# Sixteen products of every chunk summed on TensorE instead of on GpSimd and VectorE, in a graph network with a selective scan

## The reference, cut to what matters

```
h = relu(adj @ x @ gcn_w + gcn_b); h = layernorm(h) * ln_g + ln_b
xz = h @ w_in;  xc, z = xz[:, :256], xz[:, 256:]
u = silu(causal_conv4(xc) + conv_b)
dbc = u @ w_xp                      # 8 ranks, 16 of B, 16 of C
dt = softplus(dbc[:, :8] @ w_dt + b_dt)
dA = exp(dt[:, :, None] * A);  dBu = dt[:, :, None] * B[:, None, :] * u[:, :, None]
def step(hst, inp):                 # hst: 256 channels x 16 states
    dAt, dBut, Ct = inp
    hst = dAt * hst + dBut
    return (hst, hst @ Ct)          # sum over 16 states of state * C
_, ys = lax.scan(step, zeros, (dA, dBu, C))
out = x + ((ys + u * D_skip) * silu(z)) @ w_out
```

## Time and profile before

| what | value |
| --- | --- |
| median of 3 runs | 2748.58 us (2747.08 to 2750.45) |
| the profiled execution, its own time | 2750.08 us |
| its span in the profile | 2748.1 us |
| PE busy | 2307.8 us (84%) |
| DVE busy | 2213.9 us (81%) |
| ACT busy | 1033.1 us (38%) |
| POOL busy | 977.4 us (36%) |
| first L672 of slot 0 to the last scan of slot 255 | 1508.7 to 2732.0 us |

### The profile page before, as it was taken

The page is one execution under the profiler, slowest core; times in us unless marked ns, Lnnn a source line. Parts: engine busy times, 40 slices in busy tenths (PEclk is TensorE's granted clock), DMA queues, the critical chain, the costliest instruction groups (busy, mean ns, idle before and its releaser), DMA issues.

```text
span 2748.1 us, 22503 instructions
## 1 busy us (share of the span) xinstructions
PE 2307.8 (84%) x6968; PEld 1294.8 (47%) x6968; DVE 2213.9 (81%) x2409; ACT 1033.1 (38%) x1745; POOL 977.4 (36%) x409
## 2 busy tenths in 40 slices
PE   0347788999999999999999888888888988886776
PEld 0222344444458888888874344433333444333333
DVE  5889888877627666656542999999999999999997
ACT  0000000000015555555433555555555555555552
POOL 0000000000000000000000778778777787777554
PEclk9968799999999999999999999999999999997888
DMA  8999999889756555555556555555555564541111
GB/s 337 383 402 410 394 394 381 365 351 369 275 222 238 214 192 217 218 187 202 195 212 256 203 192 194 190 191 195 194 188 213 184 214 177 191 171 69 61 63 58
DMA packets 108326, 643.03 MB, mean 234 GB/s; under 512 B 14224, under 2 KB 15024, under 8 KB 42672
## 3 DMA queue, kind: packets, MB, share of 16 engines
q1 hardware_dynamic: 92160, 604.02, 57.7%
q10 hardware_dynamic: 16048, 37.57, 3.9%
HBM read 625.28 MB, written 16.25 MB: 233 GB/s over the span
## 4 chain that ended last, share of the span: by engine, by line
PE 49%; DVE 34%; issue 13%; ACT 2%; ACTq 1%; DMA 1%; POOL 0%; DVEq 0%; POOLq 0%
PE ps L853 20%; PE ps L771 12%; DVE arena L568 12%; DVE arena L686 7%; PE ps L893 6%; DVE ps L672 5%; PE ps L972 4%; PE ps L934 3%; DVE ring L686 2%; PE ps L793 2%; DVE arena L693 1%; ACTq L1002 1%; DVE arena L731 1%; DVE parts L718 1%; PE ps L914 1%
## 5 line engine op out<-in xcount | busy, mean ns | idle before, releaser
L460 POOL TENSOR_TENSOR rstd<-base,minus_half 128x8 f32<-128x8 f32 (+1 forms) x40 | 85.8, 2144 | 1492.2 <-DVE base L508 924.9
L853 PE MATMUL ps<-adj_parts,h_parts 128*128 128x512 f32 x2592 | 593.6, 390 | 2.5 <-ACT adj_parts L1068 2.1
L893 PE MATMUL ps<-ring,diag_h 128*128 128x512 f32 x1152 | 542.6, 604 | 2.1 <-DVE arena L658 2.0
L476 POOL TENSOR_TENSOR arena<-arena 128x1024 f32<-128x1024 f32 x192 | 461.4, 2409 | 230.7 <-ACT state L1135 229.7
L853 PEld LDWEIGHTS ps<-adj_parts,h_parts 128*128 128x128 f32 x2592 | 484.7, 188 | 108.8 <-ACT adj_parts L1068 4.6
L568 DVE TENSOR_TENSOR arena<-arena,ring 128x2048 f32<-128x2048 f32 x208 | 476.8, 2292 | 64.0 <-DMA ring<-adj 45.8
L771 PE MATMUL ps<-ring,arena 128*128 128x512 f32 x928 | 432.0, 626 | 64.0 <-DMA ring<-adj 64.0
L686 DVE TENSOR_TENSOR_SCAN arena<-arena,state,ps 128x512 f32<-128x512 f32 x384 | 469.4, 1264 | 1.0 <-ACT arena L1143 0.5
L1143 ACT ACTIVATE arena<-arena,a_sb 128x512 f32<-128x512 f32 x512 | 338.6, 709 | 61.7 <-DVE arena L733 61.2
L672 DVE TENSOR_TENSOR ps<-arena,ps 128x512 f32<-128x512 f32 x512 | 327.6, 685 | 19.0 <-PE ps L914 18.0
L893 PEld LDWEIGHTS ps<-ring,diag_h 128*128 128x128 f32 x1152 | 222.6, 196 | 253.2 <-issue 250.1
(11 more groups left out here) (94 smaller groups left out, 1950.6 us busy)
## 6 DMA issues: line engine op xcount, KB each, us to landing
ring<-adj SPq DMA_DIRECT2D x480, 1024.0 KB, 6.5
arena<-c_scratch SPq DMA_DIRECT2D x128, 512.0 KB, 3.8
diag_h<-adj SPq DMA_DIRECT2D x32, 1024.0 KB, 12.2
arena<-x ACTq DMA_DIRECT2D x16, 512.0 KB, 5.1
x_scratch<-arena ACTq DMA_DIRECT2D x8, 512.0 KB, 3.0
arena<-x_scratch ACTq DMA_DIRECT2D x16, 256.0 KB, 4.5
out<-arena ACTq DMA_DIRECT2D x16, 256.0 KB, 3.9
lower_scratch<-arena ACTq DMA_DIRECT2D x7, 512.0 KB, 2.6
```

Of the source, the lines that this page charges most:

```text
L476: nc.gpsimd.tensor_tensor(buf, buf, c_row, ALU.mult).then_inc(mult_done, 1)
L853: last = nc.tensor.matmul(acc[:, c, :], h_parts[:, blk % 2, layer, h_part, a * F:(a + 1) * F], adj_parts[:, buf, adj_part, c * MM:(c + 1) ...
L893: last = nc.tensor.matmul((acc_c if i else y_ps)[:, c, :], tile_of(h1, JT * s + a), blk[:, a * STRIP + c * MM:a * STRIP + (c + 1) * MM], s ...
```

## The change

POOL's pair sums (L480) and DVE's sums of pairs (L693) go, with their semaphores and the constants `QUADS`, `QUAD` and `SPARED`. POOL only multiplies by C. PE sums all sixteen buffers of every chunk, four matmuls in each even slot, as it did before in the last three chunks. The waits for a free `hs` buffer and for the finished sum count pairs now, and stand in the same slots.

```diff
-                    if g % 2 and g // 2 < PAIRS_ADDED:
-                        pool.wait_ge(mult_done, g + 1)
-                        even = hs[(g - 1) % HSB]
-                        nc.gpsimd.tensor_tensor(even, even, buf, ALU.add).then_inc(pair_done, 1)
...
-                        G = (g - HSB) // 2
-                        if added_to_next(G):
-                            dve.wait_ge(quad_done, quads_before(G + 1))
-                        else:
-                            dve.wait_ge(nsum_done, nsums_before(G + 1))
+                        dve.wait_ge(nsum_done, (g - HSB) // 2 + 1)
...
-                G, odd = divmod(g - QUAD, 2)
-                if not odd and 0 <= G < NCH * DS // 2 and added_to_next(G):
-                    dve.wait_ge(pair_done, G + 2)
-                    both = hs[(2 * G + 2) % HSB]
-                    nc.vector.tensor_tensor(both, both, hs[2 * G % HSB], ALU.add).then_inc(quad_done, 1)
...
-                    dve.wait_ge(nsum_done, nsums_before(DS // 2 * (k + 1)))
+                    dve.wait_ge(nsum_done, DS // 2 * (k + 1))
...
+                    pe.wait_ge(mult_done, 2 * G + 2)
+                    if pair == 0 and G:
+                        pe.wait_ge(y_free, G // (DS // 2))
+                    for j in range(2):
+                        for h in range(HALVES):
+                            last = nc.tensor.matmul(y_ps[:, h, :], ident[:, :], hs[(2 * G + j) % HSB][:, h, :],
+                                                    start=pair == 0 and j == 0,
+                                                    stop=pair == DS // 2 - 1 and j == 1)
+                    last.then_inc(nsum_done, 1)
```

More of the change, by code:

```diff
@@ L71 @@
 LOAD_X1, SKIP, GATE, OUT, RESIDUAL = 12, 20, 21, 25, 25
-QUADS = (1, 3)
-QUAD = 6
-SPARED = 3
 F32 = mybir.dt.float32
@@ L340, in build @@
         mult_done = sem("mult_done")
-        pair_done = sem("pair_done")
-        quad_done = sem("quad_done")
         nsum_done = sem("nsum_done")
@@ L370, in dbu_of @@
             return b_ps[g % 2] if h else first_dbu_ps
[L372 to L382, removed]
         weight_loads = [
```

## The result

| | before | after |
| --- | --- | --- |
| median of 4 runs | 2749.5 us (2747.1 to 2755.8) | 2883.8 us (2881.6 to 2889.5) |
| ratio after/before | | 1.0488, 95% interval 1.0465 to 1.0511 |
| span of the profiled execution | 2748.1 us | 2882.6 us |

The change costs 134 us. 2860 with a range of 2820 to 2890 was forecast, so the direction and the range hold and the size is 24 us short. The busy times by stretch say where the time lies: chunk 0, chunks 1 to 11, chunk 12, chunk 13, chunk 14.

The account below looks back on a forecast made before the run. DVE bounds the kernel before; PE would bound the changed one through a loop of 84.0 us plus 2.5 of half clock, 86.5 per chunk. Chunks 1 to 11 +95, with hand-overs, chunks 12 and 0 +111: 2860 us, range 2820 to 2890.

Parts of the forecast that it names:

- The coupling by one slot: PE and DVE, every slot: PE can be late by about one slot at no cost, and early by none.
- rival 1: Looser coupling, PE's work of 79.5 us per chunk bounds only on average: about 2780 us; chance 10%.
- PE's term of the loop: PE, slots 0 to 12: 61.5 instructions, 3.0 rows of B, 3.8 output and small stages, 2.5 half clock.
- the sum: Loop through PE's slots 0 to 13 and DVE's to 15: 84.0 us per chunk, 86.5 with half clock.
- DVE's term: From PE's slot 13 to the next slot 0: 1.35 + 1.7 + 8.8 + 3.8 us.
- 84 to 88 us per chunk as the sign of being right: Chunks 1 to 11 would each take this long if the forecast held.
- a shorter L731, L733 or L752 by a microsecond: DVE instructions: shortening by this much would show that POOL did matter; no gain was taken.
- The relief of VectorE: DVE's removed L693, 3.6 us per chunk: a gain only if DVE stayed the bound.
- The clock: PE behind its idle stretch before slot 0: half clock stays and adds 2.5 us per chunk.
- Chunk 12: 86.5 us plus 3.5 for the last hand-over in slot 13: 90.0 against 78.3, +12.
- Chunk 0: Slots 0 to 3 at DVE's pace, no sum in slot 4: 81 us against 76.9, +4.
- Rival 2: DVE stays the bound, sums slip into PE's waiting, pitch 0.35 us instead of 0.43: 2703 us; chance 4%.

Follow-up runs that it names:

- The kernels with the same work in two places: Kernel before plus 8 zero matmuls per chunk: in slots 14 and 15, 2753.0 us; in slots 7 and 8, 2825.0 us.
- the zero matmuls in the change's own slots: Kernel before plus the change's 20 extra matmuls per chunk, multiplying by zeros, POOL's and DVE's sums kept: 2884.0 us, ratio 1.0477.
- moving the products: Changed kernel with the products with adj spread by weights over a chunk's slots instead of evenly: 2821.0 us, 83.1 us per chunk.
- with POOL's instruction short: Changed kernel with GpSimd multiplying only the first 8 of 512 columns by C: 2814.4 us, 83.4 us per chunk.
- a small transfer of work: Kernel before without VectorE's sums of pairs, four more matmuls per chunk on TensorE: 2752.1 us; with products moved too, 2714.5 us.
- the moving alone: Kernel before with only the products with adj spread by weights over a chunk's slots: 2744.7 us, 76.4 us per chunk.

## Why the prediction was right, and where it was short

- **PE becomes the bound, by its place in the list and not by its average: right.** The coupling by one slot was the argument that set 2860 apart from rival 1's 2780. The kernels with the same work in two places show it directly (+0.1 and +6.2 us per chunk), the zero matmuls in the change's own slots reproduce the whole slowdown, and moving the products takes 5.2 us of 10.4 per chunk back.
- **PE's term of the loop: right.** In chunk 3 PE's slots 0 to 12 take 71.0 us, from the row of B before slot 0 to that of slot 13 at 1836.42; the sum had 61.5 + 3.0 + 3.8 + 2.5 of half clock = 70.8.
- **DVE's term: too small by 1.9 us, and this is the step that was mis-sized.** From PE's row of B in slot 13 to that of the next slot 0 it is 17.5 us in the mean of chunks 1 to 11, where the sum had 15.65. In chunk 3 it is 17.4, from 1836.42 to 1853.79. L701 and L726 were taken as in the rows before, 1.7 us; L669 and L694 take 1842.03 - 1838.14 = 3.9 in this chunk. Slot 14 is 0.8 shorter (7.98 against 8.8) because L699 there escapes with 1.22. That is so in six of the eleven chunks; in the five others, as in chunk 5, L694 takes 1.2, behind its 0.55 of waiting for ACT, and L699 3.1, and the term is 17.7. I asked whether GpSimd would release VectorE and answered no from L733, rightly; I didn't ask which instruction a *shifted* multiplication would now meet. The rest, 0.3 to 0.4 us, lies in slot 13 between the row of B and L669 (1.72 against 1.35): the row of B takes 0.63 there, start to start, against the 0.30 of the earlier trace rows. PE's term was 0.1 too large, so a chunk is 1.8 us over the sum, and 1.8 x 11 is 19 of the 24 us. I had named 84 to 88 us per chunk as the sign of being right; 88.3 lies just outside it. I had also named a shorter L731, L733 or L752 by a microsecond as the sign that POOL matters: none got shorter by that much in the mean, L752 got longer (1.90 to 2.91 us as L720), and POOL mattered all the same.
- **The relief of VectorE worth nothing in the changed kernel: right.** With it 88.3 us per chunk, without it 88.3.
- **The clock: right in place and size.** One drop per chunk before slot 0 stayed. Where the idle time there was shortened, the granted clock was 1.00. The Trainium skill's rule (TensorE: Matmul & The Clock Gate, "What's actually happening") is that activity releases the clock; the trace shows no release by the number of added instructions (the granted clock went from 0.94 to 0.96 only).
- **Chunk 12: right**, the sum and its parts: 90.0, with 70.4 us on PE and 19.6 from there to slot 0, where 70.8 and 19.15 were forecast. Chunk 0's 81.0 came out by luck: up to the row in slot 13 it takes 60.9 us where 63 were forecast, and from there 20.1 where the sum had 18.05.
- **Chunk 13 was taken as unchanged and cost 2.6 us.** It was put at nothing without a reason. Sums stand six slots behind their pair's first state, so pairs 5 to 7 of chunk 12 are summed in slots 0, 2 and 4 of chunk 13, with twelve instructions more. DVE waits 2.25 us for the last of them (L713, slot 4) where it waited 0.83, and its gate (L720) takes 2.92 us where it took 1.20. Other rows of the chunk go both ways.
- Slot 0 begins 1.9 us later (1510.6). Nothing is shown of it, and there may be nothing to show: in the profiled executions of the runs here whose products ahead of slot 0 stand as before, it begins between 1508.3 and 1514.9.
- Rival 2, sums cheaper for the same stationary matrix, fell with the x8 groups of 3.60 us, the same as before.

## What to carry to other kernels

Between two engines that hand each other one buffer per step, spare time is only worth something in the steps where it lies: add up the work by steps along the loop, with one step of slack, before you move work to the engine that looks idle on average. Then move the filler (here the products that no one waits for) into the steps where the other engine is long; that made a small transfer of work pay that was worth nothing without it (74.7 us per chunk against 78.2, and 76.4 by the moving alone). When instructions of GpSimd shift in time, look also at which instructions of VectorE they will now meet, and which of the two begins first.

## What the runs showed of the hardware that I had not expected

A VectorE instruction with two SBUF inputs and a GpSimd multiplication hold each other up, and not in proportion: the one that begins first keeps its length, and the other ends about one own length behind it. So a few tenths of a microsecond decide which of them pays. In the six chunks of the changed kernel in which POOL began 0.09 us before softplus, L694 took 3.36 us and POOL 2.36; in the five in which it began 0.14 us behind, L694 took 1.22 and POOL 3.30. L701, which POOL's multiplication preceded by 0.73 us, took 3.25 in every chunk; with POOL's instruction short, all of them took 1.2. The scans, which have one input in PSUM, stayed at 1.26 us with and without GpSimd's traffic. And the price of this contention on the loop was more than its own length (4.8 against 4.1 us per chunk), since it also lengthened TensorE's wait before slot 0 and with it the half clock behind it.
